# First feed-forward layer and centring as split fp32r products, with new orders on all engines

## The reference

```
for i in range(DEPTH):                                  # 6 layers
    x = attn_layer(shift_tokens(x), Wqkv[i], ...) + x   # 16 heads of 64, windows of 32, q and k normalised and rotated
    x = ffn_layer(shift_tokens(x), g, bln, W1, b1, W2, b2) + x

def ffn_layer(x, g, bln, W1, b1, W2, b2):
    mu = x.mean(-1, keepdims=True)
    var = ((x - mu) ** 2).mean(-1, keepdims=True)
    xn = (x - mu) / jnp.sqrt(var + 1e-05) * g + bln
    hg = xn @ W1 + b1                                   # 128 -> 2 * 341
    a, gate = jnp.split(hg, 2, -1)
    return a * gelu(gate) @ W2 + b2                     # 341 -> 128
```

## Time and profile before

| | |
|---|---|
| median of 3 runs | 1719.82 us (1713.82 to 1723.14) |
| profiled execution, first to last instruction (span) | 1711.8 us; its time with what lies around the span is not recorded apart, the three runs lie 2.0 to 11.3 us above the span |
| PE busy | 1660.6 us, 97% of the span |
| DVE busy | 1480.6 us, 86% |
| POOL busy | 1283.8 us, 75% |
| ACT busy | 1268.7 us, 74% |
| share of PE in the chain that ended last | 80% |

### The profile page before, as it was taken

The page is one execution under the profiler, slowest core; times in us unless marked ns, Lnnn a source line. Parts: engine busy times, 40 slices in busy tenths (PEclk is TensorE's granted clock), DMA queues, the critical chain, the costliest instruction groups (busy, mean ns, idle before and its releaser), DMA issues.

```text
span 1711.8 us, 65044 instructions
## 1 busy us (share of the span) xinstructions
PE 1660.6 (97%) x26531; PEld 1330.2 (78%) x26531; DVE 1480.6 (86%) x2313; ACT 1268.7 (74%) x2639; POOL 1283.8 (75%) x1744
## 2 busy tenths in 40 slices
PE   7999959999999999999999999999999999999997
PEld 5777637878888888888788888888878887888885
DVE  6887748989999999999889999999989898999984
ACT  6888746767777777777777777777777777777774
POOL 7787568777777877777778777787877777777770
PEclk9999979999999999999999999999999999999999
DMA  3588516564866656765567756658565567656654
GB/s 123 189 289 315 183 37 150 123 149 105 241 136 147 147 116 152 207 158 135 125 141 196 168 138 137 143 121 236 123 161 127 132 142 205 155 132 138 143 119 118
DMA packets 101385, 265.43 MB, mean 155 GB/s; under 512 B 26720, under 2 KB 34912, under 8 KB 101088
## 3 DMA queue, kind: packets, MB, share of 16 engines
q1 hardware_dynamic: 101088, 261.26, 60.6%
HBM read 45.15 MB, written 27.26 MB: 42 GB/s over the span
## 4 chain that ended last, share of the span: by engine, by line
PE 80%; issue 2%; SPq 1%; DVE 1%; ACT 1%; POOL 1%; DMA 1%; ACTq 0%; DVEq 0%; POOLq 0%
PE ps L1784 12%; PE ps L1801 10%; PE ps L1786 10%; PE ps L1842 10%; PE ps L1785 10%; PE ps L1821 8%; PE ps L1892 7%; PE ps L1831 5%; PE ps L1903 4%; PE ps L1814 2%; SPq L1228 1%; PE ps L1861 1%; PE ps L1869 1%; PE ps L1853 1%; PE ps L1878 1%
## 5 line engine op out<-in xcount | busy, mean ns | idle before, releaser
L1312 POOL TENSOR_TENSOR rot<-rot 128x512 f32<-128x512 f32 x380 | 480.7, 1287 | 99.6 <-DVE rot L1411 99.6
L1411 DVE TENSOR_TENSOR rot<-ps,rope_l 128x1024 f32<-128x1024 f32 x380 | 463.3, 1221 | 48.2 <-ACT sq L1568 33.4
L1578 ACT ACTIVATE un<-ps 128x512 f32<-128x512 f32 x384 | 229.5, 598 | 238.1 <-PE ps L1786 205.3
L1784 PE MATMUL ps<-w_t,xs_hi 128*128 128x512 f32 x764 | 377.4, 494 | 19.2 <-PEq L362 11.0
L1355 POOL TENSOR_TENSOR rot<-rot,rnorm 128x1024 f32<-128x1024 f32 x190 | 362.1, 1906 | 21.4 <-POOL rnorm L1339 0.4
L1786 PE MATMUL ps<-w_t,xs_lo 128*128 128x512 f32 x764 | 303.4, 397 | 0.4 <-issue 0.4
L1785 PE MATMUL ps<-w_t,xs_hi 128*128 128x512 f32 x764 | 301.5, 395 | 1.6 <-issue 1.6
L1568 ACT ACTIVATE sq<-ps 128x512 f32<-128x512 f32 x380 | 227.0, 601 | 60.3 <-PE ps L1786 59.9
L1397 DVE TENSOR_REDUCE ssum<-sq 128x16 f32<-128x1024 f32 x190 | 230.8, 1215 | 27.4 <-ACT sq L1568 27.4
L1801 PE MATMUL ps<-ident_s,rot 128*128 128x128 f32 x1536 | 236.9, 277 | 3.3 <-ACT kT L1594 1.7
L1801 PEld LDWEIGHTS ps<-ident_s,rot 128*128 128x128 f32 x1536 | 178.5, 140 | 52.1 <-issue 22.6
(11 more groups left out here) (139 smaller groups left out, 3013.9 us busy)
## 6 DMA issues: line engine op xcount, KB each, us to landing
vk<-un SPq DMA_DIRECT2D x1440, 128.0 KB
w_t<-weights_dram SPq DMA_DIRECT2D x48, 512.0 KB, 6.5
weights_dram<-rot SPq DMA_DIRECT2D x12, 1024.0 KB, 5.2
weights_dram<-sq SPq DMA_DIRECT2D x24, 512.0 KB, 4.3
raw<-wqk_dram SPq DMA_DIRECT2D x24, 256.0 KB, 4.5
wvt_s<-wvt_dram SPq DMA_DIRECT2D x12, 256.0 KB, 5.3
wo_s<-wo_dram SPq DMA_DIRECT2D x12, 256.0 KB, 5.8
w_s<-w_dram SPq DMA_DIRECT2D x6, 341.0 KB
```

Of the source, the lines that this page charges most:

```text
L1312: last = G.tensor_tensor(cos[:, :, s, :], cos[:, :, s, :], sin[:, :, 1 - s, :], ALU.add)
L1411: V.tensor_tensor(dst, src[:, None, :, :].broadcast_to([P, 2, H // 2, D]), tab[:, :, None, :].broadcast_to([P, 2, H // 2, D]), ALU.mult).t ...
L1578: S.activation(un[:, (u[1] % 2) * TT + t, j // 2, (j % 2) * HALF:(j % 2 + 1) * HALF], ps[:, PJ + PJ_BANK[t][QK_BANKS + j], :], ACT.Copy).t ...
L1784: M.matmul(bank, x_hi, w_t[:, j, 0, :], start=True, stop=False)
```

## The change

1. `feed_w1`: each float32 matmul of 256 columns becomes three fp32r matmuls of 256 columns (high x high, high x low, low x high). ACT makes the high part of the input (`feed_hi`), POOL the low part (`feed_lo`). W1 is split once a layer in the same two functions, in the unit with n % 8 = 5 of the layer before (for layer 0 in unit 0), into double buffers; `load_w1` moves to an earlier place on SP.
2. `feed_mean` and `feed_2`: the mean and the subtraction become one product with a centring matrix, as two fp32r matmuls of 256 columns with the high and low part of x. ACT makes the high part (`residual_hi`), DVE the low part (`residual_lo`); ACT copies the centred result out of PSUM (`copy_center`), and `square_x` reads PSUM.
3. The lists of all engines are new, and so are `PJ_BANK`, `PJ_BEFORE` and the order of the weight renewals. `turn` and `norms` are cut into smaller entries, and the reciprocal after `soft_sum` stands apart.

```diff
-        PJ_BANK = ((0, 1, 0, 1, 0, 0, 1, 1), (1, 0, 1, 0, 1, 0, 1, 0))
+        PJ_BANK = ((0, 1, 0, 1, 0, 1, 0, 0), (1, 0, 1, 0, 1, 0, 1, 1))
...
+        def split_layer(n):
+
+            return 0 if n == 0 else n // B + 1 if n % B == 5 and n // B < L - 1 else None
...
+                def feed_lo(u):
...
+                    pool.wait_ge(xgh_a.sem, xgh_a.at(n))
+                    G.tensor_tensor(xg_lo[:, :], xg[:, :], xg_hi[:, :], ALU.subtract).then_inc(xgl_g.sem, 1)
+                    layer = split_layer(n)
+                    if layer is not None:
...
+                        G.tensor_tensor(w1_lo[:, layer % 2, :], w1_s[:, :], w1_hi[:, layer % 2, :], ALU.subtract).then_inc(w1l_g.sem, 1)
...
-                    dve.wait_ge(mean_p.sem, mean_p.at(n))
-                    V.tensor_tensor(xc[:, :], xT[:, bass.ds((n % B) * XW, T)], ps[:, FB, 0:T], ALU.subtract).then_inc(xc_d.sem, 1)
+                def residual_lo(u):
...
+                    dve.wait_ge(x2h_a.sem, x2h_a.at(n))
+                    V.tensor_tensor(x2_lo[:, :], xT[:, bass.ds((n % B) * XW, T)], x2_hi[:, :], ALU.subtract).then_inc(x2l_d.sem, 1)
...
+                def residual_hi(u):
...
+                    act.wait_ge(x2_d.sem, x2_d.at(n))
+                    S.activation(x2_hi[:, :], xT[:, bass.ds((n % B) * XW, T)], ACT.Copy).then_inc(x2h_a.sem, 1)
...
+                def copy_center(u):
...
+                    act.wait_ge(mean_p.sem, mean_p.at(n))
+                    S.activation(xc[:, :], ps[:, FB, 0:T], ACT.Copy).then_inc(xc_a.sem, 1)
...
+                def feed_hi(u):
...
+                    act.wait_ge(xh_a.sem, xh_a.at(n))
+                    S.activation(xg_hi[:, :], xg[:, :], ACT.Copy).then_inc(xgh_a.sem, 1)
...
-                    M.matmul(ps[:, FB, 0:T], mean_w[:, :], xT[:, bass.ds((n % B) * XW, T)], start=True, stop=True).then_inc(mean_p.sem, 1)
+                    M.matmul(ps[:, FB, 0:T], center[:, :], x2_hi[:, :], start=True, stop=False)
+                    M.matmul(ps[:, FB, 0:T], center[:, :], x2_lo[:, :], start=False, stop=True).then_inc(mean_p.sem, 1)
...
-                        last = M.matmul(ps[0:rows, feed_bank(n, i), g * T:(g + 1) * T], w1_s[:, g * DI + at:g * DI + at + rows], xg[:, :],
-                                        start=True, stop=True)
...
+                        M.matmul(bank, w_hi, xg_hi[:, :], start=True, stop=False)
+                        M.matmul(bank, w_hi, xg_lo[:, :], start=False, stop=False)
+                        last = M.matmul(bank, w_lo, xg_hi[:, :], start=False, stop=True)
```

More of the change, by code:

```diff
@@ L1506, in step @@
                 def step(m, s):
-                    after, u, before, last, oldest = ((m, s + k) for k in (1, 0, -1, -2, -3))
-                    rope(u, 0, 1, 0)
+                    after, u, before, last = ((m, s + k) for k in (1, 0, -1, -2))
                     rope(u, 0, 1, 1)
                     soft_sum(before, 0)
-                    feed_4(oldest)
-                    soft_top(before, 1)
                     feed_1(last)
-                    soft_shift(before, 1)
-                    feed_2(last)
+                    soft_reciprocal(before, 0)
+                    residual_lo(last)
                     if index(last) == UNITS - 1:
@@ L1539, in step @@
                     soft_scale(before, 1)
+                    feed_hidden(last, 1)
                     soft_shift(u, 0)
                     rope(after, 0, 0, 0)
-                    feed_hidden(last, 1)
                     rope(after, 0, 0, 1)
+                    feed_hidden(last, 2)
                     sums(after, 0, 0)
-                    feed_hidden(last, 2)
+                    rope(after, 0, 1, 0)
                     sums(after, 0, 1)
+                    feed_4(last)
                 pipeline(dve, step)
@@ L1915, in step @@
                     after, u, before, last = ((m, s + k) for k in (1, 0, -1, -2))
+                    transpose_qk(before, 1, 1, 1)
+                    values(last, 1)
+                    proj(u, 0, 4)
+                    if index(last) == UNITS - 1:
+                        keep_warm(8, TP)
+                    transpose_o(last)
+                    proj(u, 1, 4)
+                    scores(before, 1)
+                    proj(u, 1, 5)
+                    proj(u, 0, 5)
                     if index(last) == UNITS - 2:
@@ L1953, in step @@
                     feed_w1(last, 1)
+                    transpose_qk(u, 1, 0, 0)
+                    proj(u, 1, 7)
                     proj(after, 0, 0)
-                    transpose_qk(u, 1, 0, 0)
+                    transpose_qk(u, 1, 0, 1)
                     proj(after, 0, 1)
+                    feed_w1(last, 2)
                     transpose_p(before, 1)
-                    transpose_qk(u, 1, 0, 1)
                     proj(after, 0, 2)
-                    feed_w1(last, 2)
+                    transpose_qk(u, 1, 1, 0)
                     proj(after, 0, 3)
-                    transpose_qk(u, 1, 1, 0)
-                    values(before, 1)
-                    transpose_qk(u, 1, 1, 1)
                     if index(last) == UNITS - 1:
```

239 lines of the change are left out of this document (152 added, 87 removed).

## The result

The changed kernel takes 1744.38 us (median of 4 runs, 1742.95 to 1745.23), the kernel before 1718.98 us beside it (1713.82 to 1723.14). The ratio is 1.0154 [1.0132, 1.0177]: 1.5% slower. The profiled execution took 1742.95 us with a span of 1741.2, so 1.75 us lie around the span; the span grew by 29.4 us.

A forecast was written before the change was run, and what follows sets the result against it. PE was taken as the bound: 0.61 us a unit saved, less 0.10 us where engines meet, over 46 units gives 23 us; 1719.8 - 23 + 3 us of drain, stated as 1701 us. Range 1688 to 1732 us.

The forecast's parts named there:

- 1719.8 - 23 + 3: Whole kernel: time before, less 23 us saved over 46 units, plus 3 us of longer drain.
- 1719.8 - 37 + 3: Low end of the forecast's own range: 0.11 us a matmul, no loss where engines meet; stated as 1687 us.
- the way of DVE to `residual_lo`: DVE's work from the last sum of squares until it reaches `residual_lo`, put at 4.65 us, inside POOL's `normalise`.
- the bounds 0.11 and 0.19: PE, fp32r matmul of 256 columns: 0.11 us saves 0.8 us a unit, 0.19 us loses 0.8 us.
- The rival in which loads don't overlap: PE's short matmuls: at 0.19 us each, PE takes 0.8 us a unit more, 1760 us; chance 5%.
- The forced waits of DVE: DVE waits its new list makes unavoidable: 0.35, 0.6, 0.4 and 0.5 us a unit, bringing 27.2 to 29.05 us.
- `residual_lo` comes, of the same size: 27.2 us stay: DVE: `residual_lo` replaces `feed_2` at the same 0.41 us, so work stays 27.2 us a unit.
- my rival, at 30%: DVE's `residual_lo`, both inputs in SBUF, waits 0.9 us for POOL's instruction to end: 1727 us, 1712 to 1740; chance 30%.
- I cost this at nothing, with 2 us to either side: SP's reordered weight loads at layer boundaries: no cost, within 2 us either way.
- Its 3 us of drain: End of the kernel: feed-forward chain grows about 1.5 us a unit for the last one or two, 3 us.
- The split of W1, put at nothing,: Once a layer on POOL and ACT: hidden by POOL's 5 us free a unit; without cover at most 10 us.
- DVE can follow, with nothing to spare: DVE's unit of 29.05 us lies just below PE's 29.2 us, so DVE keeps up.

The follow-up runs named there:

- Experiment 1: The changed kernel, but ACT also copies x into the free half of the feed-forward PSUM bank and `residual_lo` reads it there: 1717.15 us, ratio 1.0009.
- experiment 6: The kernel before plus one unused 128x256 DVE subtraction a unit ahead of `feed_2`, both inputs in SBUF: 1746.62 us, ratio 1.0158.
- Experiment 7: The kernel before plus one unused 128x256 DVE subtraction a unit ahead of `feed_2`, second input in PSUM: 1731.34 us, ratio 1.0078.
- experiment 5: Experiment 1 with ACT's second `exps` moved back to its earlier place, behind `square(before, 1, 0, 1)`: 1714.81 us, ratio 0.9984.
- experiment 9: Experiment 5 with `proj(u, 1, 7)` ahead of tile 1's first `transpose_qk` on PE, and one pair swapped on ACT: 1715.40 us, ratio 0.9984.
- Experiments 10 to 12: Already-met wait instructions put ahead of the units on PE: 128 in the kernel before, 1734.52 us; 64 and 128 in experiment 5, 1715.20 and 1724.66 us.

## Why the prediction was wrong

The forecast of 1701 us and its sign were wrong, and the time is above the range as well. (Three sums are off by a little and change nothing: 1719.8 - 23 + 3 is 1699.8 and was stated as 1701, 1719.8 - 37 + 3 is 1685.8 and not 1687, and the way of DVE to `residual_lo` adds up to 4.6 and not 4.65 us.) By its own steps:

- **PE: right.** The short form costs 0.119 us where I took 0.12; the bounds 0.11 and 0.19 were far apart, and the argument from the two records of a float32 matmul found the value. `feed_w1` takes 2.14 us of PE a unit, the centring 0.24, so PE saved 0.63 us; I had 0.61. The rival in which loads don't overlap did not occur. The rule of the Trainium skill, TensorE: Matmul & The Clock Gate, section "Part 3: Packing small matmuls — row/col tiling", would have put 0.19 us of load on top of the stream; this trace disagrees with it at 0.119 us for both.
- **The forced waits of DVE: right.** `lsum` 0.6 us a unit (22.4 / 38; I had 0.6), `hid` 0.3 (0.4), the sums of squares and ropes 0.4 together (0.5), `x_lo` for ACT 0.2 (0.35).
- **The step that failed: "`residual_lo` comes, of the same size: 27.2 us stay".** It is 1.79 us and not 0.41, so DVE's unit is 27.2 + 1.38 + about 1.5 of waits, 30.1, which is the measured unit. The mechanism was my rival, at 30%. Experiment 1 shows that it is the cause (27 us come back when the operand lies in PSUM), and experiments 6 and 7 show it apart from this change. The rule of the Trainium skill, SBUF — State Buffer, section "SBUF: two separate sides", states it; the trace now agrees, with 1.79 us against 0.42. I had put it at 30% since the trace of before had no such pair. That it had none among some 32 DVE operations a unit was itself a hint I passed over. The fixed 0.28 us behind POOL's instruction, in 46 units here and 36 in experiment 6, leaves no room for an operation that is merely slow.
- **Its size: too small.** I reckoned a wait of 0.9 us from the middle of a `normalise` of 1.9. But DVE gets there 0.4 us into it, and the wait was 1.38 on the mean, with the longest 2152 - 424 = 1.7. It is nearly the same point in each unit: 0.26 to 0.44 us into the `normalise` in 45 of the 46. The reason is argued and not tried: what frees DVE to reach `residual_lo` (rope, sum, `feed_1`) runs in step with the norm steps of POOL.
- **A cost that I put at nothing: the pauses of PE.** "I cost this at nothing, with 2 us to either side" spoke only of one weight bank. The pauses over 0.5 us without a releaser rose from 3.9 to 18.6 us in the two profiled executions, and the units lost some 15 us beyond the undisturbed length, the split of W1 included. The rival's 1727 us had 0.1 us a unit where 0.27 came, and nothing for these 15. Its 3 us of drain were about right: 4 us after the last projection.
- **The split of W1, put at nothing,** costs 1.3 to 1.6 us in a unit with a split, some 7 us in all five, within the 10 us of its "at most". "POOL has 5 us free in the unit" was no cover: PE waits for ACT twice, behind the 0.76 us copy of W1's high part, and then for DVE.
- **DVE's reserve.** "DVE can follow, with nothing to spare" was too kind even without the lock. Experiment 1 removes it and the median unit is 29.69 us, not 29.2; moving a wait (experiment 5) gains 0.08 us, moving a transpose (experiment 9) 0.04 more. Experiment 7 says why: an idle DVE of 2.6 us a unit had room for almost none of 0.41 us more.

**What the pauses are.** The page counts a DMA queue that carries instructions:

```profile
q8 instruction: 214, 3.51, 0.9%
```

That is 214 packets of 16 KB, one in 8 us. I set the pauses of all 14 profiles against its packets. Of the 124 pauses over 0.7 us, 120 end 1.08 to 1.60 us after such a packet has ended (median 1.39); the four others stand in experiment 6, where PE waits for ACT. Among the 120 are five that the views put down to ACT or to a load of a weight bank, the 1.9 us of the earlier trace rows among them. By chance some 7 in 100 would fall so. So PE most likely waits for its own code and goes on when a packet has landed, though the profile does not say whose instructions a packet carries. Experiments 10 to 12 show that the pauses lie elsewhere when the code does.

**What stays open.** What makes one packet come late and most in time, so that the 120 pauses sum to 5.9 us in one profile and 19.4 in another, and how much this sum varies between executions of one kernel. The effect of the code's place without the 8 to 15 us at the start was not measured. Why experiment 6 lies 6 us further above experiment 7 than its longer records explain is open as well; the pauses over 0.5 us in it are 16.1 against 6.7 us, which would cover it, but 4.0 of them are waits for ACT, and its profiled execution lay 4 us above its median.

No version beats the kernel before by more than 0.2%. The fastest are experiment 5 with 64 extra waits (0.9981) and experiments 5 and 9 (0.9984), 1.7% below the changed kernel.

## What to carry to other kernels

Before a two-input operation is added on DVE, look at where both inputs lie: with one in PSUM it takes its time, with both in SBUF it also takes what is left of POOL's instruction, and that shows in the record's length and in no wait. A saving on the busiest engine is worth only what the next one can follow, and the second engine's idle time is no reserve when it consists of waits that the lists force; put one dummy operation on it and read what it costs. Where a kernel's gain is under 1%, sum up PE's pauses that have no releaser in both profiles: here they differ by 15 us of 1741 between two profiles. And look at how far a profiled execution lies from its median: here 5 us, a third of that difference. A boundary that is read from one operation moves with that operation's place in the list; take two before a start or a drain is given a cost.

## What the hardware showed that I had not expected

- A DVE subtraction 128x256 with both inputs in SBUF lasts 415 to 2152 ns beside a busy POOL, and where it has to wait it ends 0.28 us after POOL's instruction; with one input in PSUM it lasts 408 to 426 ns in every unit.
- An fp32r matmul with 256 columns and its load of 128 columns takes 0.119 us, half of the 0.23 of one with 512.
- PE pauses of 0.7 to 4.9 us come in every version, in sum 5.9 to 19.4 us, and end 1.1 to 1.6 us behind a packet of the instruction queue. With 128 instructions that do nothing ahead of the units they were 11.2 instead of 5.9 us, in one profile each.
- Such an instruction, a wait for a semaphore that is long there, follows the one before it on PE by 0.11 us (median), though nothing is left to wait for.
